# Layer 0's preparation in a score bank, and GpSimd splitting the maxima, in a two-layer gated cross-attention kernel

## The chip, the cores and the metric

The kernel runs on one core of one Trainium2 chip. The metric is the time of one execution on the device in microseconds. 2429.8 us is the median of three runs of the kernel before.

## What is computed

Two layers, each a cross-attention followed by a mixture of experts, over 32 batches of 56 query tokens of width 128 and 1500 context tokens. The attention of layer 0 has 32 heads of width 4 (16 pairs, whose outputs are subtracted), that of layer 1 has 16 heads of width 8 and a mask. Cut to what matters here:

```
x = x + tanh(g_xattn[0]) * L0_xattn(layernorm(x), ctx, ctx)
x = x + tanh(g_ffn[0])   * L0_ffn(layernorm(x))
x = x + tanh(g_xattn[1]) * L1_xattn(layernorm(x), ctx, ctx, mask)
x = x + tanh(g_ffn[1])   * L1_ffn(layernorm(x))

L0_xattn:  q = query @ Wq.T; k = ctx @ Wk.T; v = ctx @ Wv.T
           p = softmax(q * SCALE @ k.T) per head (32 heads, 1500 keys)
           attn = p1 @ v - lam * (p2 @ v), divided by its root mean square per head, @ Wp.T + bp
```

All numbers are kept nearly exact: a float32 value goes to TensorE as a high and a low float16 part.

## The kernel before, in words

`attend` (line 476) writes the attention of a layer for all engines, with an order laid down by hand. For a batch n of layer 0 it goes through 12 steps t of 125 keys each. A step consists of:

- the **scores** (`scores`, line 894) in two halves h of 16 heads each, 8 matmuls in all, into `score_ps[0]` and `score_ps[1]` (two banks each); the row maximum is subtracted by two extra rows of the operands;
- the exponentials on ScalarE (`exps`, line 1007), one instruction of 125x896 for each half, out of `score_ps` into `probs`;
- the **weighing** of the values (`weigh`, line 916) with the exponentials of the step before, in two halves i, into `acc_ps`, which holds the sum over all keys until ScalarE copies it out (`copy_output`, line 1015) in step 0 of the next batch;
- the **search** of the maxima of a later batch (`search`, line 880): 4 pieces of 112 queries by 500 keys in two pairs, each into one bank; VectorE reduces each to a column (`reduce_piece`, line 1056). 48 pieces make the maxima of a batch;
- one **preparation** (`use`, line 838, emptied by `drain`, line 979) for another batch: T turns a third of the context (n+3), K projects a third of the keys (n+3), V a third of the values (n+2), M transposes the maxima (n+1), F turns half of the output and A transposes the finished attention (n-1). K, T and the like are emptied by ScalarE; M is split into its high and low part by VectorE (lines 1043 and 1045).

The table `where` (line 553) says in which step, and on which side of the second search pair, a preparation stands. TensorE's order in a step is: both halves of the scores, first search pair, half of the weighing, preparation, second search pair, the other half of the weighing.

Searches and preparations share three banks, `spare_ps`, `max_ps[0]` and `max_ps[1]`, strictly in turn (`rooms`, line 593; `room`, line 597). A user waits until the user three places ahead has been emptied (`wait_for_room`, line 832):

```python
                k = place_of[user]
                if k >= len(rooms):
                    pe.wait_ge(*drained(order[k - len(rooms)]))
```

GpSimd prepares queries, splits context and keys into parts, and combines the outputs of the batch before (`finish`, line 771) once VectorE has written the reciprocals, which it does one step after the second F. SP issues the transfers in one queue: among them the transfer of the maxima into their two operand rows (`fill_m`, line 664, 4 transfers), behind the store of the context parts and ahead of that of the keys. The scores of step 0 of a batch wait for these rows (line 898).

Layer 1 runs the same code with half the heads (one half of scores, 2 pieces a step) and a mask.

## Time and profile before

| | |
|---|---|
| runs shown | 2422.18, 2429.8, 2433.78 us |
| the profiled execution | 2424.42 us; span from first to last instruction 2422.6 us |
| TensorE busy | 2235.1 us, 92% of the span |
| VectorE, ScalarE, GpSimd busy | 71%, 61%, 51% |
| granted TensorE clock, mean | 0.949 of 2.4 GHz |
| layer 0's attention | from about 100 to 1300 us of the span |

The profile lists for each engine what it executed and when, counted in us from the span's start. A stretch of it can be asked for in order of time. Consecutive instructions of one kind are merged there into one row with their number; the duration of such a row reaches to the end of its last. Matmuls are pipelined, and their ends are modelled, so that neighbouring rows of TensorE overlap; what can be read from them best is the distance from start to start. An idle time in brackets is that of the engine just ahead of the row, with what ended it.

### The profile page before, as it was taken

The page shows a single profiled execution, that of the slowest core. Times are in us where ns is not written, and L with a number is a line of the kernel's source. Part 1 is how long each engine was busy: PE and PEld are TensorE (multiplying, and loading weights), DVE is VectorE, ACT ScalarE, POOL GpSimd, SP SyncE. Part 2 cuts the span into 40 slices and gives each one's busy share as a digit, 9 for nine tenths or more (in the row PEclk, how much of TensorE's full clock was granted, in tenths as well). Part 3 has the DMA queues.
Part 4 walks back from the last instruction along what each step waited for, and adds up shares of the span by engine and source line. Part 5 has one row for each costly group of instructions (what it writes and reads, how often), then busy time and mean ns, then how long its engine had stood idle before and what let it go on. Part 6 is the DMA issues. An engine that isn't in the chain of part 4 may idle for free. (4 is left out here: it accounts for less than half of the span.)

```text
span 2422.6 us, 67012 instructions
## 1 busy us (share of the span) xinstructions
PE 2235.1 (92%) x27256; PEld 1258.2 (52%) x27256; DVE 1720.9 (71%) x3761; ACT 1484.6 (61%) x2101; POOL 1247.5 (51%) x1322
## 2 busy tenths in 40 slices
PE   3899999999999999999996986999999999999798
PEld 2344444444444444444444763566666655666576
DVE  3778888888888888888872554766777766775544
ACT  3167777777777777777774432566777666767322
POOL 5234545545455454454523344666777666773232
PEclk9589999999999999999997996899999999999799
DMA  3624343443444434434311006666676675762100
GB/s 108 128 71 103 88 92 103 87 105 85 99 103 93 92 98 92 104 85 94 91 13 51 23 29 135 125 133 130 141 142 137 136 137 122 142 136 41 53 1 15
DMA packets 113419, 227.80 MB, mean 94 GB/s; under 512 B 46052, under 2 KB 58596, under 8 KB 112612
## 3 DMA queue, kind: packets, MB, share of 16 engines
q1 hardware_dynamic: 113124, 223.67, 41.8%
q8 instruction: 209, 3.42, 0.7%
q14 instruction: 86, 0.70, 0.1%
HBM read 146.77 MB, written 76.48 MB: 92 GB/s over the span
## 5 line engine op out<-in xcount | busy, mean ns | idle before, releaser
L1012 ACT ACTIVATE probs<-score_ps 125x896 f32<-125x896 f32 x1152 | 1014.1, 916 | 368.9 <-PE score_ps L911 368.0
L1070 DVE TENSOR_REDUCE max_part<-max_ps 112x1 f32<-112x500 f32 x1023 | 665.4, 672 | 129.9 <-PE max_ps L890 89.9
L927 PE MATMUL acc_ps<-probs,vext 125*32 125x224 f32 (+1 forms) x12288 | 680.5, 317 | 4.3 <-issue 3.6
L890 PE MATMUL max_ps<-kstack,qstack 48*112 48x500 f16 x1534 | 512.3, 407 | 23.8 <-ACT kstack L987 11.1
L1067 DVE CUSTOM_DVE_ANT_0 kstack<-max_ps,kstack 112x500 f32<-112x500 f32 x511 | 335.3, 675 | 142.2 <-PE max_ps L890 83.4
L927 PEld LDWEIGHTS acc_ps<-probs,vext 125*32 125x32 f32 x12288 | 258.7, 109 | 272.9 <-issue 266.3
L1070 DVE TENSOR_REDUCE max_part<-spare_ps 112x1 f32<-112x500 f32 x513 | 344.8, 672 | 78.2 <-PE max_ps L890 45.6
L911 PE MATMUL score_ps<-qstack,kstack 50*125 50x224 f16 (+1 forms) x6144 | 389.8, 244 | 4.3 <-ACT probs L1012 2.1
L911 PEld LDWEIGHTS score_ps<-qstack,kstack 50*125 50x125 f16 x6144 | 306.4, 135 | 154.2 <-issue 122.4
L890 PE MATMUL spare_ps<-kstack,qstack 48*112 48x500 f16 x770 | 312.4, 406 | 30.0 <-issue 16.7
L767 POOL CAST khl<-kstack 128x500 f16<-128x500 f32 x189 | 113.6, 601 | 350.4 <-ACT kstack L994 194.1
L890 PEld LDWEIGHTS max_ps<-kstack,qstack 48*112 48x112 f16 x1534 | 168.0, 129 | 150.9 <-DVE max_part L1070 88.4
L1067 DVE CUSTOM_DVE_ANT_0 kstack<-spare_ps,kstack 112x500 f32<-112x500 f32 x257 | 173.5, 675 | 85.1 <-PE max_ps L890 77.1
L769 POOL TENSOR_TENSOR khl<-kstack,khl 128x500 f16<-128x500 f32 x189 | 202.2, 1070 | 15.1
L784 POOL TENSOR_TENSOR heads_out<-turned,rden 56x64 f32<-56x64 f32 x192 | 55.5, 289 | 241.2 <-DVE rden L1053 231.2
L1396 POOL TENSOR_TENSOR kstack<-kstack,probs 112x512 f32 (+1 forms) x68 | 90.6, 1333 | 171.2 <-DVE probs L1343 171.2
L905 PE MATMUL score_ps<-kstack 56*125 56x448 f16 x768 | 158.5, 402 | 0.2 <-issue 0.2
L747 POOL TENSOR_SCALAR kstack<-mask_in 112x1500 bf16<-112x1500 uint8 x31 | 147.2, 4747 | 2.6
L744 POOL TENSOR_SCALAR kstack<-mask_in 120x1500 f16<-120x1500 uint8 x31 | 147.8, 4768 | 0.0
L890 PEld LDWEIGHTS spare_ps<-kstack,qstack 48*112 48x112 f16 x770 | 99.0, 129 | 92.1 <-DVE max_part L1070 42.6
L736 POOL TENSOR_TENSOR qstack<-qrows,wide 112x896 f16<-112x896 f16 (+1 forms) x64 | 83.8, 1310 | 47.4 <-DMA qrows<-q_parts 25.4
L1243 PEld LDWEIGHTS max_ps<-kstack 128*112 128x112 f32 x896 | 104.4, 177 | 5.1 <-issue 0.2
(203 smaller groups left out, 2621.8 us busy)
## 6 DMA issues: line engine op xcount, KB each, us to landing
kstack<-k_parts SPq DMA_DIRECT2D x384, 187.5 KB, 6.6
k_parts<-khl SPq DMA_DIRECT2D x128, 375.0 KB, 2.8
ctx_f<-in_ctx SPq DMA_DIRECT2D x32, 750.0 KB
ctx_f<-context_parts SPq DMA_DIRECT2D x32, 750.0 KB, 4.5
context_parts<-ctx_f SPq DMA_DIRECT2D x16, 750.0 KB, 3.4
context_parts<-kstack SPq DMA_DIRECT2D x16, 750.0 KB, 3.3
mask_in<-in_mask SPq DMA_DIRECT2D x128, 82.0 KB
qrows<-q_parts SPq DMA_DIRECT2D x384, 7.0 KB, 7.4
```

What stands on the lines that cost most here:

```text
L744: nc.gpsimd.tensor_scalar(by_chunk(mask_f[n % SLOTS][0:HALF + SQ, :]), turned_keys(mask_in[0:HALF + SQ, :]), -BIG, None, ALU.mult).then_in ...
L747: nc.gpsimd.tensor_scalar(by_chunk(mask_add[n % SLOTS]), turned_keys(T["mask_in2"][:, :]), -BIG * BIG, None, ALU.mult).then_inc(s_add, 1)
L767: nc.gpsimd.tensor_copy(khl[:, 0, k], key_f[:, k]).then_inc(s_kp, 1)
L769: nc.gpsimd.tensor_tensor(khl[:, 1, k], key_f[:, k], khl[:, 0, k], ALU.subtract).then_inc(s_kp, 1)
L890: nc.tensor.matmul(room(("P", n, p))[0:PIECE, 0:TK], qstack[n % SLOTS][rows, c, PIECE * i:PIECE * (i + 1)], kstack[n % SLOTS][rows, c, TK ...
L905: nc.tensor.matmul(buf[0:KT, r, 0:448], mask_f[n % SLOTS][HALF * r:HALF * r + SQ, keys], big_eye[HALF * r:HALF * r + SQ, :], start=True, s ...
L911: last = nc.tensor.matmul(buf[0:KT, r, GC * k:GC * (k + 1)], kstack[n % SLOTS][rows, h * here + k, keys], qstack[n % SLOTS][rows, h * here ...
L927: last = nc.tensor.matmul(acc_ps[32 * j:32 * j + 32, TT * S * i:TT * S * (i + 1)].rearrange("p (s c) -> p s c", s=S), vext[n % SLOTS][:, t ...
L1012: nc.scalar.activation(probs[t % 2][:, 896 * h:896 * h + 896].rearrange("k (b c) -> k b c", b=2), score_ps[(t * H + h) % 2][0:KT, :, 0:448 ...
L1067: nc.vector.tensor_tensor_reduce(masked_scores[p % 2], scores, mask_add[n % SLOTS][:, TK * third:TK * third + TK], 1.0, -3.0e38, ALU.add, ...
L1070: nc.vector.reduce_max(best, scores, AX.X).then_inc(s_red, 1)
L1243: last = nc.tensor.matmul(bank[4 + e % DB - (0 if gated else 1)][0:TT, D * t:D * t + D], hidden[(e * NF + f) % HS][:, TT * t:TT * t + TT], ...
```

## The change

Only layer 0 is touched:

- All preparations of layer 0 stand behind the second search pair and ahead of the second half of the weighing. Each writes into one of the two banks of the score buffer of its own step's first half (`in_scores`), once that half's exponentials have been read out, and no longer takes a turn in the three rotating banks. Step 0 has none; T, F, T, F, T, K stand one step later than before, M and V share step 7, A and V step 11.
- The second half of the scores comes behind the first search pair. It waits until the preparation of the step before has been emptied. In odd steps the halves swap (`halves_of`), so that the first half of a step takes the buffer of the second half of the step before, and waits for both exponentials of that step.
- In step 0 both halves of the weighing come ahead of the second search pair.
- The transposed maxima are copied out by ScalarE, scaled, into a strip of `mask_in2`, which layer 0 does not use; GpSimd splits them in three instructions, behind the first third of the key split. `fill_m` waits for that.

```diff
-        where = {("T", 0): (0, 1), ("F", 0): (1, 1), ("T", 1): (2, 1), ("F", 1): (3, 1), ("T", 2): (4, 1), ("K", 0): (5, 1),
-                 ("V", 0): (6, 1), ("M", 0): (7, 1), ("K", 1): (8, 1), ("V", 1): (9, 1), ("K", 2): (10, 1), ("V", 2): (11, 1),
-                 ("A", 0): (11, 2)}
+        where = {("T", 0): (1, 1), ("F", 0): (2, 1), ("T", 1): (3, 1), ("F", 1): (4, 1), ("T", 2): (5, 1), ("K", 0): (6, 1),
+                 ("M", 0): (7, 1), ("V", 0): (7, 1), ("K", 1): (8, 1), ("V", 1): (9, 1), ("K", 2): (10, 1), ("A", 0): (11, 1),
+                 ("V", 2): (11, 1)}
...
+    spare_uses, in_scores = list(first_preps) + [("M", 0, 0)], {}
     for n in range(B):
         for t in range(NKT):
-            order += searched(n, t, 0) + at_step(n, t, 1) + searched(n, t, 1) + at_step(n, t, 2)
+            middle, last = at_step(n, t, 1), at_step(n, t, 2)
+            spare_uses += middle + last
+            if H == 2:
+                in_scores.update({user: n * NKT + t for user in middle})
+                middle = []
+            order += searched(n, t, 0) + middle + searched(n, t, 1) + last
...
+    def halves_of(step):
+
+        return (0, 1) if step % 2 == 0 or H == 1 else (1, 0)
 
     def room(user):
 
         if user in place_of:
             return rooms[place_of[user] % len(rooms)]
+        if user in in_scores:
+            return score_ps[halves_of(in_scores[user])[0]][:, int(user[0] in "MA"), :]
...
             def fill_m(n):
-                sp.wait_ge(s_mr, n + 1)
+                sp.wait_ge(s_mr, n + 1 if L.masked else 3 * (n + 1))
...
+            def split_max(n):
+                pool.wait_ge(s_mc, n + 1)
+                high, low = max_rows[0:L.tiles, 0, 0:PIECE], max_rows[0:L.tiles, 1, 0:PIECE]
+                nc.gpsimd.tensor_copy(high, max_f).then_inc(s_mr, 1)
+                pool.wait_ge(s_mr, 3 * n + 1)
+                nc.gpsimd.tensor_tensor(max_rest, max_f, high, ALU.subtract).then_inc(s_mr, 1)
+                pool.wait_ge(s_mr, 3 * n + 2)
+                nc.gpsimd.tensor_scalar(low, max_rest, BIG, None, ALU.mult).then_inc(s_mr, 1)
...
                 if n + 3 < B:
-                    split_keys(n + 3)
+                    split_keys(n + 3, range(1))
+                if L is L0 and n + 1 < B:
+                    split_max(n + 1)
+                if n + 3 < B:
+                    split_keys(n + 3, range(1, NTHIRD))
...
+                if user in in_scores:
+                    pe.wait_ge(s_exp, in_scores[user] * H + 1)
...
-            def scores(n, t, h):
-                number = (n * NKT + t) * H + h
-                at_least(pe, s_exp, number - 1)
-                if t == 0 and h == 0:
+            def scores(n, t, place):
+                step = n * NKT + t
+                number = step * H + place
+                h = halves_of(step)[place]
+                if L.masked:
+                    at_least(pe, s_exp, number - 1)
+                elif place == 0:
+                    at_least(pe, s_exp, number)
+                else:
+                    at_least(pe, s_exp, number - 2)
+                    for user in in_scores:
+                        if in_scores[user] == step - 1:
+                            pe.wait_ge(*drained(user))
...
-                    for h in range(H):
-                        scores(n, t, h)
+                    weighed = (n, t - 1) if t else (n - 1, LAST)
+                    scores(n, t, 0)
                     search(searched(n, t, 0))
+                    if H == 2:
+                        scores(n, t, 1)
                     for i in range(2):
-                        if t:
-                            weigh(n, t - 1, i)
-                        elif n:
-                            weigh(n - 1, LAST, i)
-                        if i == 0:
+                        if i == 1 and (t or H == 1):
+                            search(searched(n, t, 1))
                             for user in at_step(n, t, 1):
                                 use(user)
-                            search(searched(n, t, 1))
+                        if weighed[0] >= 0:
+                            weigh(*weighed, i)
+                    if t == 0 and H == 2:
+                        search(searched(n, t, 1))
...
+                if kind == "M":
+                    at_least(act, s_mr, 3 * n)
+                    nc.scalar.activation(max_f, spare_ps[0:L.tiles, 0:PIECE], ACT.Copy, scale=1.0 / BIG).then_inc(s_mc, 1)
```

How this moves instructions. First TensorE in step 8 of batch 1, which prepares keys, and the start of step 9. The names are those of the banks and buffers with their numbers: `score_ps` rows of 125x224 are scores, rows of 112x500 searches, `acc_ps` rows the weighing, and the row of 128x500 x3 the keys. Before:

```order
L911 MATMUL score_ps0<-qstack1,kstack1 125x224 x4
L911 MATMUL score_ps1<-qstack1,kstack1 125x224 x4
L890 MATMUL spare_ps<-kstack0,qstack0 112x500
L890 MATMUL max_ps0<-kstack0,qstack0 112x500
L927 MATMUL acc_ps<-probs1,vext1 32x224 x4
L857 MATMUL max_ps1<-ctx_f,w_parts 128x500 x3
L890 MATMUL spare_ps<-kstack0,qstack0 112x500
L890 MATMUL max_ps0<-kstack0,qstack0 112x500
L927 MATMUL acc_ps<-probs1,vext1 32x224 x4
```

With the change:

```order
L954 MATMUL score_ps0<-qstack1,kstack1 125x224 x4
L923 MATMUL max_ps1<-kstack0,qstack0 112x500
L923 MATMUL spare_ps<-kstack0,qstack0 112x500
L954 MATMUL score_ps1<-qstack1,kstack1 125x224 x4
L970 MATMUL acc_ps<-probs1,vext1 32x224 x4
L923 MATMUL max_ps0<-kstack0,qstack0 112x500
L923 MATMUL max_ps1<-kstack0,qstack0 112x500
L890 MATMUL score_ps0<-ctx_f,w_parts 128x500 x3
L970 MATMUL acc_ps<-probs1,vext1 32x224 x4
```

The fourth search shares its bank with the second one of its step before (`max_ps0`), and with the first one in the change (`max_ps1`). The keys leave the rotating banks for the bank of the first scores.

Second, TensorE at the start of a batch, steps 0 and 1 of batch 2 (the rows of 128x125 x4 turn the context). Before:

```order
L878 MATMUL max_ps0<-wide,attn_n 128x56
L911 MATMUL score_ps0<-qstack2,kstack2 125x224 x4
L911 MATMUL score_ps1<-qstack2,kstack2 125x224 x4
L890 MATMUL max_ps1<-kstack0,qstack0 112x500
L890 MATMUL spare_ps<-kstack0,qstack0 112x500
L927 MATMUL acc_ps<-probs1,vext1 32x224 x4
L848 MATMUL max_ps0<-wide,ctx_f 128x125 x4
L890 MATMUL max_ps1<-kstack0,qstack0 112x500
L890 MATMUL spare_ps<-kstack0,qstack0 112x500
L927 MATMUL acc_ps<-probs1,vext1 32x224 x4
```

With the change:

```order
L954 MATMUL score_ps0<-qstack2,kstack2 125x224 x4
L923 MATMUL spare_ps<-kstack0,qstack0 112x500
L923 MATMUL max_ps0<-kstack0,qstack0 112x500
L954 MATMUL score_ps1<-qstack2,kstack2 125x224 x4
L970 MATMUL acc_ps<-probs1,vext1 32x224 x8
L923 MATMUL max_ps1<-kstack0,qstack0 112x500
L923 MATMUL spare_ps<-kstack0,qstack0 112x500
L954 MATMUL score_ps1<-qstack2,kstack2 125x224 x4
```

Step 0 has no preparation any more, its weighing is in one piece, and two searches with nothing but four scores between them and the next two end it.

Third, GpSimd between the combination of a batch's output and the next preparation of queries: the splits of the last third of the context and of the keys, before:

```order
L798 TENSOR_TENSOR attn_n<-attn,rms 56x128
L756 CAST ctx_f<-kstack 128x500
L758 TENSOR_TENSOR ctx_f<-kstack,ctx_f 128x500
L767 CAST khl<-kstack 128x500
L769 TENSOR_TENSOR khl<-kstack,khl 128x500
L767 CAST khl<-kstack 128x500
L769 TENSOR_TENSOR khl<-kstack,khl 128x500
```

With the change, the numbers of the buffers written out:

```order
L823 TENSOR_TENSOR attn_n<-attn,rms 56x128
L772 CAST ctx_f<-kstack0 128x500
L774 TENSOR_TENSOR ctx_f<-kstack0,ctx_f 128x500
L792 CAST khl<-kstack1 128x500
L794 TENSOR_TENSOR khl<-kstack1,khl 128x500
L779 CAST max_rows<-mask_in2 16x112
L781 TENSOR_TENSOR mask_in2<-mask_in2,max_rows 16x112
L783 TENSOR_SCALAR max_rows<-mask_in2 16x112
L792 CAST khl<-kstack1 128x500
L794 TENSOR_TENSOR khl<-kstack1,khl 128x500
```

Three small instructions stand behind the first third of the keys; the two that VectorE had for this are gone from its order.

## Rows read from the trace of the kernel before

**Rows 1.** Busy time by stretch, one batch: us, then PE, PEld, DVE, ACT, POOL, clock

```profile
608.35:645.77 37.42, 36.37 (x406) 17.30 (x407) 31.04 (x54) 27.15 (x37) 18.66 (x27) 1.00 0.37 96
```

**Rows 2.** In order of time, PE, a step with keys: start, us, work

```profile
602.24 0.60 PE L911 MATMUL score_ps<-qstack,kstack 50*125 50x224 f16 x8
602.68 0.37 PE L890 MATMUL max_ps<-kstack,qstack 48*112 48x500 f16 x1
...
602.98 0.58 PE L927 MATMUL acc_ps<-probs,vext 125*32 125x224 f32 x8
603.50 0.81 PE L857 MATMUL max_ps<-kstack,w_parts 128*128 128x500 f16 x3
604.24 0.41 PE L890 MATMUL max_ps<-kstack,qstack 48*112 48x500 f16 x1
604.40 0.41 PE L890 MATMUL spare_ps<-kstack,qstack 48*112 48x500 f16 x1
604.75 0.59 PE L927 MATMUL acc_ps<-probs,vext 125*32 125x224 f32 x8
605.26 0.60 PE L911 MATMUL score_ps<-qstack,kstack 50*125 50x224 f16 x8
```

**Rows 3.** In order of time, ACT: exponentials, the last two rows five steps apart

```profile
602.69 1.73 ACT L1012 ACTIVATE probs<-score_ps 125x896 f32<-125x896 f32 x2 [0.67 <-PE score_ps L911]
...
615.72 1.73 ACT L1012 ACTIVATE probs<-score_ps 125x896 f32<-125x896 f32 x2 [0.96 <-PE score_ps L911]
...
630.83 1.73 ACT L1012 ACTIVATE probs<-score_ps 125x896 f32<-125x896 f32 x2 [0.67 <-PE score_ps L911]
```

**Rows 4.** In order of time, PE: values, then context, each with the search behind it

```profile
606.52 0.91 PE L864 MATMUL spare_ps<-w_parts,ctx_f 128*125 128x128 f16 x12
607.36 0.48 PE L890 MATMUL max_ps<-kstack,qstack 48*112 48x500 f16 x2
...
616.53 0.65 PE L848 MATMUL max_ps<-wide,ctx_f 125*128 125x125 f32 x4
617.11 0.42 PE L890 MATMUL max_ps<-kstack,qstack 48*112 48x500 f16 x1
```

**Rows 5.** In order of time, DVE: the second reduction of the step in rows 2

```profile
603.68 0.67 DVE L1070 TENSOR_REDUCE max_part<-spare_ps 112x1 f32<-112x500 f32 x1
```

**Rows 6.** In order of time, ACT and PE, step 1 of a batch

```profile
612.01 0.58 ACT L987 ACTIVATE kstack<-spare_ps 128x500 f32<-128x500 f32 x1
...
612.64 0.41 PE L890 MATMUL spare_ps<-kstack,qstack 48*112 48x500 f16 x1 [0.61 <-ACT kstack L987]
```

**Rows 7.** In order of time, PE, near the end of layer 0's attention

```profile
1266.36 0.41 PE L911 MATMUL score_ps<-qstack,kstack 50*125 50x224 f16 x4 [0.20 <-ACT probs L1012]
1266.70 0.96 PE L927 MATMUL acc_ps<-probs,vext 125*32 125x224 f32 x16
1267.59 0.27 PE L878 MATMUL max_ps<-wide,attn_n 56*128 56x56 f32 x1
```

**Rows 8.** In order of time, ACT, the last batch

```profile
1276.55 13.71 ACT L1012 ACTIVATE probs<-score_ps 125x896 f32<-125x896 f32 x16 [0.27 <-PE score_ps L911]
```

**Rows 9.** In order of time, POOL: the combination, and the key split behind it

```profile
623.77 1.40 POOL L784 TENSOR_TENSOR heads_out<-turned,rden 56x64 f32<-56x64 f32 x4 [3.96 <-DVE rden L1053]
625.27 0.60 POOL L791 TENSOR_SCALAR attn<-heads_out,lam_s 56x128 f32<-56x128 f32 x1
...
634.04 1.07 POOL L769 TENSOR_TENSOR khl<-kstack,khl 128x500 f16<-128x500 f32 x1
```

**Rows 10.** In order of time, SP's queue: the rows of the maxima

```profile
633.83 3.07 SPq L670 DMA_DIRECT2D qstack<-max_rows  x4
```

**Rows 11.** DMA issues of the page: count, KB each, median us to landing

```profile
kstack<-k_parts SPq DMA_DIRECT2D x384, 187.5 KB, 6.6
k_parts<-khl SPq DMA_DIRECT2D x128, 375.0 KB, 2.8
...
qrows<-q_parts SPq DMA_DIRECT2D x384, 7.0 KB, 7.4
```

More of the change, by code:

```diff
@@ L533, in attend @@
     s_mr = sem(L.name + "_max_split")
+    s_mc = s_mr if L.masked else sem(L.name + "_max_copied_out")
+    max_f, max_rest = (T["mask_in2"][0:L.tiles, 4 * PIECE * i:4 * PIECE * (i + 1)].bitcast(F32) for i in range(2))
     s_os = sem(L.name + "_output_copied")
@@ L758, in split_context, with split_keys @@
                 nc.gpsimd.tensor_tensor(ctxT[n % 2][:, 1, k], context_f[:, k], ctxT[n % 2][:, 0, k], ALU.subtract).then_inc(s_cp, 1)
-            def split_keys(n):
-                for i in range(NTHIRD):
+            def split_max(n):
[6 more added lines that the diff above has]
+                nc.gpsimd.tensor_scalar(low, max_rest, BIG, None, ALU.mult).then_inc(s_mr, 1)
+            def split_keys(n, thirds=range(NTHIRD)):
+                for i in thirds:
                     k = slice(TK * i, TK * i + TK)
@@ L814, in _ @@
             split_keys(2)
+            if L is L0:
+                split_max(0)
             for n in range(B):
@@ L980, in drain @@
                 kind, n, i = user
-                if kind == "M":
+                if kind == "M" and L.masked:
                     return
@@ L1017, in copy_output @@
                 nc.scalar.activation(out_sb[:, 0:L.o_cols], acc_ps[:, 0:L.o_cols], ACT.Copy).then_inc(s_os, 1)
-            for user in first_preps:
+            for user in first_preps + [("M", 0, 0)]:
                 drain(user)
@@ L1037, in drain @@
                 kind, n, i = user
-                if kind != "M":
+                if kind != "M" or not L.masked:
                     return
```

16 lines of the change are left out of this document (10 added, 6 removed).

## The prediction, made before the changed kernel had run

> **What bounds the kernel now.** I read the stretches first, then one batch of layer 0 on TensorE, ScalarE and VectorE in order of time, then GpSimd, the DMA queue and the stage's end. The edit touches only layer 0's attention; layer 1 gets the same instructions in the same order, as do the norms and the feed-forwards, so their time is taken as unchanged. In one batch (12 steps) TensorE is busy 36.37 of 37.42 us, VectorE 31.04, ScalarE 27.15, at a granted clock of 1.00, the 2.4 GHz level [rows 1]. That reads like "TensorE is full", and it misleads. Follow the step that prepares keys [rows 2]: scores 602.24, first search pair 602.68, half of the weighing 602.98, keys 603.50, then the second pair as two separate starts, 604.24 and 604.40, weighing 604.75, next scores 605.26: 3.02 us. ScalarE's pairs of exponentials show the same length for five steps in a row, 615.72 to 630.83 being 15.11 [rows 3], though their preparations differ: on TensorE the keys take 0.74, the values 0.84, turning the context 0.58 [rows 2, 4]. A constant length with unequal contents is a loop, not a full engine. The loop: four users share three banks, so a preparation pushes the fourth search of a step (604.40, in spare_ps) onto the bank of the step's second search. It starts 0.05 after that one's reduction ends, 603.68 + 0.67 = 604.35 [rows 5]. Add it up: 0.35 to the weighing, 0.51 to the next scores, 0.44 to the next pair, some 0.4 until that is in its bank, two reductions of 0.6 to 0.67, and the next fourth search may start: 3.0 us. All other work lies in the loop's slack.
>
> Twice in a batch it is worse. In step 1 the first search waits 0.61 idle for ScalarE, which empties its bank of the context turned in step 0 only at 612.01, behind the copy of the accumulator [rows 6]. In step 7 the transposed maxima hold a bank until VectorE has split them. What these two and the transpose of the attention cost is 37.42 - 12 x 3.02 = 1.2.
>
> **The change, part by part, for one batch.** *Banks.* The three rotating banks hold searches alone. The fourth search then waits for the first one's reduction, 0.6 earlier, and no search waits for ScalarE. What is late next is TensorE itself, so its starts must be summed. *Split scores.* Eight scores and a pair took 0.44 + 0.30 before the weighing [rows 2]. Now: half of the scores, 0.22; the pair ahead of the other half, not in the trace, nearest the pair ahead of the weighing, 0.30; four scores ahead of a weighing, 1266.36 to 1266.70, 0.34 [rows 7]. That is 0.86 for 0.74. Bounds: nothing extra, since the streams are the same; or a full change of work at both new seams. What such a change costs: both weighing halves together take 0.89 (1266.70 to 1267.59), two apart 2 x 0.52, so 0.15 [rows 2, 7]; then 0.74 + 0.30 = 1.04. I stay with the nearest rows, 0.86. *The rest of a step.* Weighing half 0.52; second pair ahead of the preparation 0.35, as 604.40 to 604.75; preparation; weighing half 0.51: with the 0.86, 2.24 without preparation. Eleven of these are 24.6. Three keys, three values, three contexts at 0.74, 0.84, 0.58 and two output turns, taken like the context, are 2.2 + 2.5 + 2.9 = 7.6. The transposes of maxima and attention are single matmuls of 0.27 [rows 7], pipelined: between 0 and 0.27 each, 0.1 taken. Step 0, without preparation: 0.86 + 0.52 + 0.51 + 0.30 = 2.2. But VectorE needs 31.04 / 48, 0.63 a reduction, 2.5 for its four, and step 0's second pair comes behind both weighing halves, so step 1's first searches find banks unread: some 0.6 of waiting. Sum 24.6 + 7.6 + 0.2 + 2.2 + 0.6 = 35.2. I add 0.3 for small waits that a sum of starts does not see, and take **35.5 us for 37.42**, 1.9 less.
>
> *ScalarE* gains one copy of 16x112. Exponentials start 0.45 after the scores, two take 1.73, a drain 0.58 [rows 2, 3, 6]: 2.3 to 2.6 of steps of 2.8 to 3.1. Two new waits. A preparation waits for the first exponentials of its own step, done at 0.45 + 0.9 = 1.4 (a little over half of the 1.73); TensorE comes at 0.86 + 0.52 + 0.35 = 1.7: nothing, margin 0.3. The second half of the scores waits for the preparation's drain, done 3.1 to 3.2 after its step's start and wanted at 2.8 to 3.1 plus 0.52: nothing, margin 0.2 to 0.3. Both are thin, and TensorE's whole queue would stand behind them.
>
> *VectorE* loses the split of the maxima and its wait. It isn't the bound, and the wait in step 7 is already left out of the sum.
>
> *The first scores of a step* wait for both exponentials of the step before, where one sufficed, since the halves swap banks. Cycle: 1.73 + 0.05 + 0.45 = 2.2 us, covered as long as VectorE's 2.5 bounds a step. Not covered in the last 17 steps, in which nothing is searched (5 of batch 30, 12 of batch 31): there ScalarE runs 16 exponentials in 13.71, 1.71 a step [rows 8]. Up to 17 x 0.5 = 8.7 is lost; some of these steps are longer already by output turns and a copy, so 7 is taken.
>
> *GpSimd and the queue.* The second output turn moves from step 3 to step 4, so the reciprocals come in step 5, by the sum some 16.3 after the batch's start. From the start of the combination to the end of the first third of the key split it takes 634.04 + 1.07 - 623.77 = 11.3 [rows 9], to 27.6. Then the three new instructions of 16x112: none like them is in the trace; nothing up to the 0.60 of the 56x128 row each [rows 9], 1.5 taken with their links, the upper end: 29.1. On SP stand behind them four row transfers, 3.07 to issue [rows 10], the last at 31.6, and then the key store, which needs the last third and isn't delayed. Their landing is not in the trace: 2.8 for the key store and 7.4 for the query rows bound it [rows 11]. The 7.4 stand behind six key fills; these have one context store ahead of them, so I take 2.8: 34.4. The next batch's scores come at 35.5: nothing, with 1 us to spare where 6.7 were (633.83 + 2.5 + 2.8 against 645.77). The other two thirds of the key split move back by 1.5, into idle time.
>
> *Total.* Batches 1 to 28 are full ones: 28 x 1.9 = 53. Batch 0 runs partly at the lower clock level and batch 29 has few preparations; nothing is taken for them. 2424.4 - 53 + 7 = 2378 against the profiled execution; the median of the runs shown is 5 us higher and would give 2384. **Forecast: 2380 us.**
>
> **Rivals.** (a) *The split costs nothing.* For: a pair follows eight scores after 0.44, and the 0.22 of four is just half of that. Against: the pair ahead of the weighing takes 0.30 where a preparation hides nothing of it. It would be 0.12 x 12 = 1.4 less, 34.1 a batch: 2424 - 28 x 3.3 + 7 = 2339. The Trainium skill (TensorEngine Tiling, Key Properties) says that changing the tiling mode, not just the tile, drains the engine. By that rule the split is free, as scores (50 rows) and searches (48 rows) lie in the same halves of the array. No row here shows the new seam itself.
>
> (b) *The seams eat it.* With 1.04 for 0.86 a batch is 35.5 + 2.2 = 37.7, and TensorE is the bound it seems to be: 2424 + 8 + 7 = 2439; with half of that, 2408. For: busy 36.4 of 37.4. Against: the constant 3.02.
>
> (c) *The maxima come late, and it is slower than before.* Their path now ends on GpSimd behind the combination. If the last row lands 7.4 after its issue, at 39.0, the scores of each batch wait 3.5, and a batch is 39.0: 2424 + 28 x 1.6 + 7 = 2476. It costs from a landing of 3.9 on and turns the sign near 5.5. For: the margin shrinks from 7 to 1, and a 7.4 exists. Against: that one has 1.1 MB of key fills ahead of it.
>
> **How the numbers follow.** Forecast case 0.62, (a) 0.12, (b) 0.14, (c) 0.12. A measurement of this kernel tells 0.5%, 12 us, from no change. Faster by more: 0.62 + 0.12 + a third of (b) = 0.78; within: 0.07; slower: (c) and the far end of (b), 0.15. The forecast's own range is 2362 to 2400 (35.0 to 36.2 a batch). For 8 in 10 the range reaches to (a) and into (b), 2335 to 2430, and leaves (c) out.
>
> **What would show it.** Accumulator copies 35.5 us apart; steps of unequal length by their preparation, 2.8 for the context, 3.0 to 3.1 for keys and values; no search waiting for ScalarE, and few for reductions outside steps 0 and 1; the split on GpSimd followed at once by four row transfers, and the first scores of a batch without a gap; ScalarE idle 0.5 a step in the last 17. Equal steps near 3 us would mean a new loop. A gap ahead of a batch's first scores is (c). Unequal steps, each 0.15 longer than summed, are (b).

## The result, and the profile after

The changed kernel takes 2349.4 us, the median of 4 runs (2344.1 to 2361.7), and the kernel before beside it 2426.0 (4 runs): a ratio of 0.970, 95% interval 0.968 to 0.972. The profiled execution took 2361.7 us, the longest of the four, with a span of 2359.2, beside 2424.4 and 2422.6 before. A batch of layer 0, read from one copy of the accumulator to the next, is 35.01 us where it was 37.42. The figure that decides below is this batch length: within one profile of the changed kernel it repeats to 0.02 us, while the totals of single runs differ by several us. The window of one batch, columns as in [rows 1]:

```profile
610.04:645.05 35.01, 34.84 (x408) 18.66 (x404) 29.61 (x51) 27.93 (x39) 19.66 (x30) 1.00 0.45 102
```

TensorE is busy in 34.84 of 35.01 us, almost as in [rows 1], although the batch is 2.4 us shorter. Its row looks the same when it is full and when it stands in a loop. In order of time, TensorE, one step with a context third (step 3), then the first reductions of that step on VectorE:

```profile
618.27 0.41 PE L954 MATMUL score_ps<-qstack,kstack 50*125 50x224 f16 x4
618.51 0.37 PE L923 MATMUL spare_ps<-kstack,qstack 48*112 48x500 f16 x1
618.51 0.37 PE L923 MATMUL max_ps<-kstack,qstack 48*112 48x500 f16 x1
618.73 0.35 PE L954 MATMUL score_ps<-qstack,kstack 50*125 50x224 f16 x4
619.01 0.58 PE L970 MATMUL acc_ps<-probs,vext 125*32 125x224 f32 x8
619.53 0.41 PE L923 MATMUL max_ps<-kstack,qstack 48*112 48x500 f16 x1
619.65 0.41 PE L923 MATMUL spare_ps<-kstack,qstack 48*112 48x500 f16 x1
620.00 0.65 PE L881 MATMUL score_ps<-wide,ctx_f 125*128 125x125 f32 x4
620.58 0.58 PE L970 MATMUL acc_ps<-probs,vext 125*32 125x224 f32 x8
621.09 0.41 PE L954 MATMUL score_ps<-qstack,kstack 50*125 50x224 f16 x4
```

```profile
618.92 0.68 DVE L1119 TENSOR_REDUCE max_part<-spare_ps 112x1 f32<-112x500 f32 x1 [0.37 <-PE max_ps L923]
619.52 1.25 DVE L1119 TENSOR_REDUCE max_part<-max_ps 112x1 f32<-112x500 f32 x2
```

Three things stand here. The scores, the pair and the other scores take 0.24, 0.22 and 0.28 us, 0.74 to the weighing, exactly as long as eight scores and a pair in [rows 2]. The two searches of the second pair start 0.12 apart, since the fourth waits for the first reduction (618.92 + 0.68 = 619.60). From the pair's start to the preparation it is 0.47. The steps are no longer equal: in order from step 0, with what TensorE prepares in each,

| | 0 | 1 | 2 | 3 | 4 | 5 | 6 | 7 | 8 | 9 | 10 | 11 |
|---|---|---|---|---|---|---|---|---|---|---|---|---|
| before | T 3.14 | F 3.84 | T 3.03 | F 3.02 | T 3.02 | K 3.02 | V 3.03 | M 3.23 | K 3.02 | V 3.02 | K 3.02 | V, A 3.03 |
| after | 2.22 | T 3.21 | F 2.80 | T 2.82 | F 2.80 | T 2.83 | K 2.99 | M, V 3.20 | K 2.99 | V 3.08 | K 2.99 | A, V 3.08 |

Step 1 keeps two waits: 0.17 of its first scores for the exponentials, and one of its second search, for the reduction that empties its bank. TensorE, where the duration 0.77 of the two searches shows that they don't start together, and VectorE's reduction, which ends at 612.81:

```profile
612.26 0.41 PE L954 MATMUL score_ps<-qstack,kstack 50*125 50x224 f16 x4 [0.17 <-ACT probs L1061]
612.51 0.77 PE L923 MATMUL max_ps<-kstack,qstack 48*112 48x500 f16 x2
612.86 0.61 PE L954 MATMUL score_ps<-qstack,kstack 50*125 50x224 f16 x4
```

```profile
612.13 0.68 DVE L1119 TENSOR_REDUCE max_part<-max_ps 112x1 f32<-112x500 f32 x1 [0.17 <-PE spare_ps L923]
```

GpSimd and then SP's queue, the split of the maxima, answering to [rows 9, 10]:

```profile
637.42 0.27 POOL L779 CAST max_rows<-mask_in 16x112 f16<-16x112 f32 x1
637.76 0.39 POOL L781 TENSOR_TENSOR mask_in<-mask_in,max_rows 16x112 f32<-16x112 f32 x1
638.24 0.49 POOL L783 TENSOR_SCALAR max_rows<-mask_in 16x112 f16<-16x112 f32 x1
```

```profile
638.75 2.69 SPq L685 DMA_DIRECT2D qstack<-max_rows  x4
```

The split ends 28.7 us into the batch (638.73), the rows are issued until 641.4, and the scores that need them start at 645.05 with no gap. In the last 17 steps ScalarE, which ran through the last eight without a pause in [rows 8], now stops 0.50 us in most, and 0.26 to 0.39 where it also empties a preparation:

```profile
1214.91 1.73 ACT L1061 ACTIVATE probs<-score_ps 125x896 f32<-125x896 f32 x2 [0.50 <-PE score_ps L954]
```

By the accumulator's copies: the first stands at 162.5 before and 157.0 after; from there 28 batches take 1047.3 and 980.3 us, 67.0 less; the three intervals to the last copy 81.6 and 87.1, 5.6 more; from the last copy to the end, in which nothing was changed, 1131.3 and 1134.8. In the other kernels of this study that keep the new preparation banks, this last part is 1121.5 to 1139.0, so some 9 us either way say nothing of the edit.

### The profile page after: what moved, and what is told of

Read it like the earlier page. It is cut to its first block and busy times, and to the rows that moved or that the text cites. A ratio compares the mean times of both kernels' runs of the same rounds, so it can differ in the third digit from the quotient of the medians.

```text
span 2359.2 us, 67435 instructions
## 1 busy us (share of the span) xinstructions
PE 2192.7 (93%) x27256; PEld 1303.0 (55%) x27256; DVE 1677.1 (71%) x3697; ACT 1507.8 (64%) x2133; POOL 1278.9 (54%) x1418
## 5 line engine op out<-in xcount | busy, mean ns | idle before, releaser
L1119 DVE TENSOR_REDUCE max_part<-max_ps 112x1 f32<-112x500 f32 x1024 | 654.7, 668 | 115.3 <-PE spare_ps L923 68.3
L970 PE MATMUL acc_ps<-probs,vext 125*32 125x224 f32 (+1 forms) x12288 | 673.2, 316 | 6.6 <-issue 6.1
L954 PE MATMUL score_ps<-qstack,kstack 50*125 50x224 f16 (+1 forms) x6144 | 454.8, 244 | 17.2 <-ACT probs L1061 13.9
L954 PEld LDWEIGHTS score_ps<-qstack,kstack 50*125 50x125 f16 x6144 | 344.4, 134 | 183.8 <-issue 122.2
L923 PEld LDWEIGHTS max_ps<-kstack,qstack 48*112 48x112 f16 x1535 | 173.5, 129 | 143.4 <-issue 77.7
L1044 ACT ACTIVATE vext<-score_ps 125x512 f32<-125x512 f32 x102 | 60.9, 597 | 78.6 <-PE score_ps L897 78.2
```

The source lines that it names most:

```text
L923: nc.tensor.matmul(room(("P", n, p))[0:PIECE, 0:TK], qstack[n % SLOTS][rows, c, PIECE * i:PIECE * (i + 1)], kstack[n % SLOTS][rows, c, TK ...
L954: last = nc.tensor.matmul(buf[0:KT, r, GC * k:GC * (k + 1)], kstack[n % SLOTS][rows, h * here + k, keys], qstack[n % SLOTS][rows, h * here ...
L970: last = nc.tensor.matmul(acc_ps[32 * j:32 * j + 32, TT * S * i:TT * S * (i + 1)].rearrange("p (s c) -> p s c", s=S), vext[n % SLOTS][:, t ...
L1119: nc.vector.reduce_max(best, scores, AX.X).then_inc(s_red, 1)
```

## The experiments

Each batch below is the distance of two accumulator copies in the middle of layer 0. Single times stand beside a kernel before of 2419 to 2425 us. e1 to e8 ran once each, e9 to e12 four to six times. The exchange of the halves and the undivided weighing of step 0 are in every kernel below that has the new banks, and in none that has the old ones, so that their own worth isn't measured.

### The parts of the change, alone and left out

**e1: VectorE splits the maxima, as before.**

```
             def drain(user):
...
-                if kind == "M" and L.masked:
+                if kind == "M":
...
-                if kind != "M" or not L.masked:
+                if kind != "M":
```

The first pair of lines is ScalarE's, which empties M no more, the second VectorE's, which splits it; GpSimd's `split_max` is not called for layer 0, and VectorE does its part behind the second reductions of step 7.

> The changed kernel, with the split of the maxima given back to VectorE (two instructions, placed behind the second reduction pair of step 7), straight from the score bank. Theory (the gain is the broken loop between reductions and searches): VectorE has 0.4 to 0.7 us of idle time in each step, 0.7 ahead of step 8, so two instructions of 0.25 fit; a batch stays at 35.0 us (34.9 to 35.2), total within 5 us of the changed kernel. Rival (taking VectorE's work away is part of the gain): a batch of 35.5 or more. The row transfers should issue about 5 us earlier in the batch, without effect.

Measured: batch 35.00, total 2356.5; the row transfers begin about 2.5 us earlier in the batch, not 5, without effect. Whether GpSimd or VectorE splits them is worth nothing once the maxima lie in a bank that no search waits for.

**e2: the kernel before, with the preparation behind the second pair, banks still in turn.**

```
                         if i == 0:
+                            search(searched(n, t, 1))
                             for user in at_step(n, t, 1):
                                 use(user)
-                            search(searched(n, t, 1))
```

The turns of the three banks and VectorE's order of emptying them follow TensorE's.

> The kernel before, with one edit: each preparation stands behind the second search pair instead of ahead of it, still in the three rotating banks; scores together as before. Theory: the fourth search then waits for the first reduction, but the scores still stand ahead of the first pair and only half of the weighing between the pairs, so that this reduction ends some 0.3 us after TensorE comes for the fourth search, and the preparation no longer fills that time: steps of about 3.0 (context, output) and 3.2 to 3.3 (keys, values), a batch of 37.0 to 37.8, no gain. Rival (the place of the preparation is what gains): a batch near 35.3, as changed.

Measured: batch 40.04, total 2504.2. The rival, a gain from the place alone, is out; the loss is larger than the theory's range. TensorE, a step with keys:

```profile
622.21 0.42 PE L890 MATMUL spare_ps<-kstack,qstack 48*112 48x500 f16 x1
622.54 0.41 PE L890 MATMUL max_ps<-kstack,qstack 48*112 48x500 f16 x1
623.12 0.81 PE L857 MATMUL max_ps<-kstack,w_parts 128*128 128x500 f16 x3 [0.17 <-DVE max_part L1070]
```

Two users wait now, each for one reduction more: the fourth search 0.33 behind the third, and then the keys, which on VectorE's row are released by two reductions that run from 621.80 for 1.26, to 623.06. In the kernel before, the 0.74 of the keys passed while the first reduction ran; with the preparation last that cover is gone. A step with keys is 3.42.

**e3: the change without the split of the scores.**

```
                     scores(n, t, 0)
-                    search(searched(n, t, 0))
                     if H == 2:
                         scores(n, t, 1)
+                    search(searched(n, t, 0))
```

> The changed kernel, with one edit: both halves of the scores ahead of the first search pair, as before; score banks for the preparations, their places and the rest stay. Theory (the second half between first pair and weighing is needed to give VectorE time for the first reduction): the fourth search waits about 0.3 us in each step, a batch of 36.8 to 37.5, nearly all of the gain gone. Rival (the score banks alone give the gain, the split costs nothing and brings nothing): 35.0 to 35.3.

Measured: batch 38.11, total 2448.9: slower than the kernel before, and a larger loss than the theory's 36.8 to 37.5. TensorE, and the drain on ScalarE that it waits for:

```profile
607.00 0.73 PE L954 MATMUL score_ps<-qstack,kstack 50*125 50x224 f16 x8
607.54 0.37 PE L923 MATMUL spare_ps<-kstack,qstack 48*112 48x500 f16 x1
...
608.39 0.41 PE L923 MATMUL max_ps<-kstack,qstack 48*112 48x500 f16 x1
608.69 0.41 PE L923 MATMUL spare_ps<-kstack,qstack 48*112 48x500 f16 x1
```

```profile
606.60 0.59 ACT L1042 ACTIVATE kstack<-score_ps 128x500 f32<-128x500 f32 x1 [0.70 <-PE score_ps L890]
```

Without the split the second scores want the preparation's bank 0.22 us after the step's start, at 607.22. It is empty at 607.19, but TensorE goes on some 0.14 behind such an end (in e5 a drain ends at 1203.71 and its scores start at 1203.85), so 0.1 is lost: scores and search take 0.54 where they took 0.44. The pair comes late, so its reduction ends late, and the fourth search waits 0.30. The split covers both.

**e4: the change with the preparation ahead of the second pair.**

> The changed kernel, with one edit: the preparation ahead of the second search pair, as before, still in the score bank. Theory: it then waits some 0.1 to 0.2 us for the first exponentials of its step, and the fourth search no longer waits 0.12 for the first reduction; the two nearly cancel: a batch of 35.0 to 35.5. Rival (the place behind the second pair is essential): 36 or more.

Its edit exchanges `search(searched(n, t, 1))` with the loop over `at_step(n, t, 1)` in steps with t > 0. Measured: batch 35.49, total 2366.4. The fourth search waits no more (both start at 608.07), but the preparation comes 0.56 behind the weighing and a search of the first pair 0.08 behind the other, and from the scores to the weighing it is 0.86 (605.92 to 606.78) for 0.74. The place behind the second pair is worth 0.5 us a batch of the 2.4.

**e11: the kernel before with the split alone.**

```
-                    for h in range(H):
-                        scores(n, t, h)
-                    search(searched(n, t, 0))
+                    scores(n, t, 0)
+                    search(searched(n, t, 0))
+                    if H == 2:
+                        scores(n, t, 1)
```

> The kernel before with one edit only: the second half of the scores behind the first search pair. Preparations keep their rotating banks and their place ahead of the second pair. Theory (the constant 3.02 us step was a loop: fourth search, weighing, next scores, next first pair, its second reduction, fourth search; the reductions count from when the first pair stands in its banks): the first pair starts 0.22 us sooner after the scores' start, so the loop is 2.80 us and TensorE's own sum takes over where that is longer (keys 2.86 to 2.9, values 2.95 to 3.0, context and output turns 2.8 from the loop); steps 1 and 7 keep their waits, 1.2 us in all; a batch is 35.3 to 36.0 us, and the total 2360 to 2385 us. Rival (the change's gain needs the preparations out of the rotating banks; a split alone only moves the wait): steps stay at 3.02 and the batch at 37.2 us or more, the total at 2415 to 2430.

Measured: batch 36.99; total 2409.0 (6 runs), ratio 0.994, 0.992 to 0.997. Neither was right on the sum: the rival had 37.2 or more and 2415 to 2430, the theory 35.3 to 36.0 and 2360 to 2385, and the result is nearer to the rival's. The steps are mostly the theory's. They are, from step 0, 3.40, 3.85, 2.83, 2.83, 2.84, 2.86, 3.08, 3.30, 2.86, 3.08, 2.98, 3.08. TensorE, first the step with keys, then step 1 of the next batch:

```profile
616.86 0.41 PE L911 MATMUL score_ps<-qstack,kstack 50*125 50x224 f16 x4
617.10 0.37 PE L890 MATMUL max_ps<-kstack,qstack 48*112 48x500 f16 x1
...
618.12 0.81 PE L857 MATMUL max_ps<-ctx_f,w_parts 128*128 128x500 f16 x3
618.86 0.41 PE L890 MATMUL max_ps<-kstack,qstack 48*112 48x500 f16 x1
618.86 0.41 PE L890 MATMUL spare_ps<-kstack,qstack 48*112 48x500 f16 x1
...
619.72 0.41 PE L911 MATMUL score_ps<-qstack,kstack 50*125 50x224 f16 x4
...
641.50 0.41 PE L911 MATMUL score_ps<-qstack,kstack 50*125 50x224 f16 x4
642.71 0.42 PE L890 MATMUL max_ps<-kstack,qstack 48*112 48x500 f16 x2 [0.81 <-ACT kstack L988]
```

The second pair starts together at 618.86, where it stood apart at 604.24 and 604.40 in [rows 2]: an earlier first pair breaks the 3.02 loop, as the theory had it. What failed is the sum over the batch. I had added the excess of steps 0, 1 and 7 over 3.02 to shorter steps; but the release of a held bank sets those steps, whatever the others take (3.14, 3.84, 3.23 before; 3.40, 3.85, 3.30 here). In the changed kernel steps 0, 1 and 7 are 8.63 together against 10.55 here: 1.9 of the 2.0 us between the two kernels.

**e12: the kernel before with the first pair ahead of all scores.**

Its edit puts `search(searched(n, t, 0))` ahead of the loop over h.

> The kernel before with the first search pair ahead of both halves of the scores, nothing else. Theory: the pair starts 0.44 us sooner, the loop would be 2.58 us, and TensorE's own sum bounds all steps (keys 2.87, values 2.97, context 2.71); the waits of steps 1 and 7 stay (the first pair of step 1 meets ScalarE's drain 0.4 us earlier, so its wait is up to 1.0 instead of 0.61); a batch is 34.8 to 35.8 us, the total 2350 to 2380. Rival (with the pair first, it waits for the reductions of the step before, which the scores had covered): the batch is 36.5 us or more.

Measured: batch 38.97; total 2474.0 (4 runs), ratio 1.021, 1.017 to 1.026. The rival is right. TensorE, the first pair of a middle step, then a later row, that of step 1:

```profile
619.16 0.41 PE L890 MATMUL max_ps<-kstack,qstack 48*112 48x500 f16 x1
619.49 0.41 PE L890 MATMUL spare_ps<-kstack,qstack 48*112 48x500 f16 x1
619.49 0.80 PE L911 MATMUL score_ps<-qstack,kstack 50*125 50x224 f16 x8
...
630.41 0.41 PE L890 MATMUL spare_ps<-kstack,qstack 48*112 48x500 f16 x1 [1.14 <-ACT kstack L990]
```

In the middle step the second search finds its bank unread, 0.33 late, and the scores stand behind it in TensorE's order, so the exponentials wait as well; in step 1 it is 1.14, for ScalarE's drain of step 0.

Together, batches in us: before 37.42; split alone 36.99; bank and place without the split 38.11; bank and split with the preparation ahead of the second pair 35.49; all 35.01. Place alone, with the banks in turn, costs 2.6; bank and place cost 0.7 without the split, and with it they gain 2.0. So the gain is no sum of the parts' gains: the bank frees the searches, and with the split TensorE no longer waits for that bank (e3). The new banks alone, with the preparation in its old place and no split, weren't run.

### How near is the split of the maxima to the scores?

**e7: the maxima behind all thirds of the keys on GpSimd.** `split_keys(n + 3)` ahead of `split_max(n + 1)`, no third behind it.

> The changed kernel, but GpSimd splits the maxima after all three thirds of the keys instead of after the first. In the changed kernel this split ends 28.7 us into the batch and the rows' four transfers are issued until 31.4; the scores that need them start at 35.0 without a wait. It isn't known how much of the 3.6 us between is slack, since the landing isn't shown by a wait anywhere. Theory (the maxima's path has about 1 us to spare or less): the thirds end about 35 us into a batch, the rows are issued until 38 and land 1.5 to 3 us later, so the batch is 39.5 to 41 us and the total about 2480 to 2520; the scores of step 0 are then released by the transfer, and the gap gives the landing. Rival (the third splits are quick or the keys' thirds wait on something that moves with them, and the path has several us to spare): the batch stays below 37 us.

Measured: 2594.3 us, batches of 40.1 to 45.0, about half of them 44.3 to 44.4. The last instruction of the split on GpSimd; the scores on TensorE that the rows release; and windows, first of the gap a batch earlier and of the time behind it, then of a batch near 40:

```profile
635.74 0.49 POOL L783 TENSOR_SCALAR max_rows<-mask_in 16x112 f16<-16x112 f32 x1
```

```profile
640.13 0.41 PE L952 MATMUL score_ps<-qstack,kstack 50*125 50x224 f16 x4 [3.99 <-DMA qstack<-max_rows]
```

```profile
591.80:595.70 3.90, 0.00 (x0) 0.00 (x0) 0.00 (x0) 0.11 (x1) 1.73 (x2) 1.00 0.05 16
...
597.00:609.00 12.00, 12.00 (x84) 4.95 (x78) 6.89 (x12) 6.23 (x9) 1.73 (x2) 0.50 0.78 118
...
426.00:429.00 3.00, 3.00 (x28) 1.40 (x25) 1.26 (x2) 2.23 (x3) 0.00 (x0) 0.50 0.69 221
```

From the end of the split (636.23) to the scores it is 3.90 us, issue included; the last of the four transfers is issued until 638.94 and is there 1.2 later. In the changed kernel the same 3.90 would end at 642.63, and the scores want it at 645.05: 2.4 us to spare. The batch is longer than the theory had it, since a second cost comes with the gap: TensorE stands still for 4.0 us, starts again at 595.78, and the granted clock is 0.67 from 596 to 597 and 0.50, the 1.2 GHz level, from 597 to 609, a search taking 0.66 in place of 0.41. That the rest of the time goes with this clock shows in a comparison of three batches whose gaps are alike and whose stretches at the low clock are not. From first scores to first scores, less the gap at the end and the 35.01 of a batch without one:

| first scores at | until | less the gap and 35.01 | clock low behind the first scores |
|---|---|---|---|
| 425.46 | 465.99 | 1.5 us | 3.4 us |
| 508.93 | 551.42 | 3.5 us | 8.9 us |
| 595.78 | 640.13 | 5.4 us | 13.6 us |

### What is left in a step, and in the tail

**e5: the last 17 steps with their halves in turn, each waiting for its own bank.**

```
-        return (0, 1) if step % 2 == 0 or H == 1 else (1, 0)
+        return (0, 1) if step % 2 == 0 or H == 1 or step >= tail else (1, 0)
...
+                elif step >= tail:
+                    at_least(pe, s_exp, number - 1)
```

> The changed kernel, but in the last 17 steps, which have no search and no preparation, the two halves of the scores are not exchanged, and each half waits only for the exponentials that last read its own bank (and for the drain of a preparation of the step before that used it). In the changed kernel these steps take 2.22 us each with ScalarE idle 0.50 us in each, since the first scores wait for both exponentials; before the change they took 1.71. Theory (that wait is what the tail lost): the batch stays at 35.0 us, the last 17 steps come back to 1.71 us (1.7 to 1.8), and the program ends 17 x 0.51 = 8.7 us earlier against a profile with the same untouched stages; against the changed kernel's total 5 to 9 us less. Rival (the tail's steps are bound by the weighing that follows its own exponentials, and the exchange has nothing to do with it): steps stay at 2.2 us and the total is the same.

Measured: batch 35.01; the last interval between copies 22.56 in place of 26.20; total 2345.4. ScalarE in the last batch:

```profile
1208.76 12.09 ACT L1069 ACTIVATE probs<-score_ps 125x896 f32<-125x896 f32 x14 [0.59 <-PE score_ps L962]
```

Fourteen exponentials without a pause, 1.73 a step. The last two intervals are 4.3 us shorter together, less than the 8.7 expected: ScalarE still stops four times in the 17 steps, 0.59 three times and 1.16 once. TensorE shows what holds it:

```profile
1197.33 0.60 PE L962 MATMUL score_ps<-qstack,kstack 50*125 50x224 f16 x8 [0.76 <-DMA qstack<-max_rows]
...
1203.85 0.60 PE L962 MATMUL score_ps<-qstack,kstack 50*125 50x224 f16 x8 [0.26 <-ACT turned L1059]
```

The 1.16 is the arrival of the last batch's maxima. The other three stand behind the emptying of a preparation: with the halves in turn the first scores of a step use the bank that the preparation of the step before had.

**e6: the first search pair ahead of both halves of the scores**, in the changed kernel.

> The changed kernel, but the first search pair of a step goes ahead of both halves of the scores, so that the order on TensorE is pair, scores, scores, weighing, pair, preparation, weighing. Theory (what is left in a step beside TensorE's own work is the 0.12 us that the fourth search waits for the first reduction): the first reduction starts 0.24 us earlier, the wait is gone, a step of keys takes 2.85 to 2.90 us instead of 2.99, and the batch 33.5 to 34.3 us; the total is some 20 to 40 us less. What could take it back: the exponentials start 0.2 us later in the step and the weighing, or the next step's first scores, then wait for them; then the batch is 35.0 or more and the rows show scores or weighing released by ScalarE in most steps. Rival (the fourth search's wait is not time lost, TensorE's own order bounds a step): 35.0.

Measured: batch 34.16, total 2324.4. TensorE, a step with keys:

```profile
616.56 0.41 PE L923 MATMUL max_ps<-kstack,qstack 48*112 48x500 f16 x1
616.57 0.41 PE L923 MATMUL spare_ps<-kstack,qstack 48*112 48x500 f16 x1
616.94 0.81 PE L890 MATMUL score_ps<-kstack,w_parts 128*128 128x500 f16 x3
...
618.19 0.42 PE L923 MATMUL max_ps<-kstack,qstack 48*112 48x500 f16 x2
618.45 0.55 PE L954 MATMUL score_ps<-qstack,kstack 50*125 50x224 f16 x8
618.93 0.58 PE L970 MATMUL acc_ps<-probs,vext 125*32 125x224 f32 x8
619.44 0.41 PE L923 MATMUL spare_ps<-kstack,qstack 48*112 48x500 f16 x1
619.45 0.41 PE L923 MATMUL max_ps<-kstack,qstack 48*112 48x500 f16 x1
```

The fourth search stands beside the third again and the step is 2.88 for 2.99. Ten steps give 1 us, and step 1 takes some back (its first pair waits 0.56 for VectorE). The same edit that cost 1.5 us a batch with the banks in turn (e12) gives 0.85 here. It also shows the price of the split once more: a pair and then eight scores take 0.26 + 0.48 = 0.74.

**e8: the preparations in the steps of the kernel before**, one of them in step 0.

> The changed kernel, but with the preparations in the steps of the kernel before: the first context transposition in step 0, the values in step 6, the maxima in step 7, behind the second pair in step 0 too. It tests the words that step 0 has none. In step 0 ScalarE has the output copy besides both exponentials, and the first scores of step 1 already wait 0.17 us for ScalarE. Theory (a preparation in step 0 costs there what it saves in another step, because its drain is one more turn of ScalarE that the second scores of step 1 wait for): step 0 or step 1 gets 0.3 to 0.6 us longer, the step that had two preparations 0.3 us shorter, and the batch is 34.8 to 35.3 us. Rival (keeping step 0 free costs a whole step's worth nowhere, the drain is hidden): the batch is 34.5 or less. Other rival (the drain collides with the copy and the exponentials in a chain): 35.6 or more.

Measured: batch 34.84, total 2356.4. Steps 0 and 1 are 2.57 and 3.10, 0.24 more than in the changed kernel, and step 7, which has M alone, is 2.51; the other ten steps together are 0.40 shorter. A step 0 without any preparation isn't worth its room: the difference is 0.17 us a batch, which the totals can't tell.

**e9: e5 and e6 together, step 1 alone in the changed kernel's order.**

> The changed kernel with the first search pair of each step ahead of both halves of the scores (as in e6), step 1 alone kept in the changed kernel's order, and the last 17 steps with the halves in turn and their own waits (as in e5). Theory (each of the two stalls is a cost of its own, so they add): the search's steps stay at e6's 2.69 to 2.88 us, step 1, whose first pair waited 0.56 us for VectorE in e6, gets 0.1 to 0.3 us shorter since scores stand where that wait was, the batch is 33.9 to 34.1 us, the last 17 steps take 1.71 to 1.75; total 2312 us (2305 to 2322), the ratio to the kernel before 0.955. Rival (step 1 waits for ScalarE or VectorE either way): the batch stays at 34.15 us and the total is 2316.

Measured: batch 34.05, last interval 22.55; total 2326.4, the median of 5 runs (2317.0 to 2327.3), ratio to the kernel before 0.958, 0.955 to 0.960. The changed kernel stands at 0.968 to 0.972: this version beats both. From the first to the last copy it takes 1036.1 us, the changed kernel 1067.4. The total came out above the range that was expected, because I had started from e6's single execution, whose part behind the last copy was 1121.5 us; here it is 1131.8.

Step 1 still stops, 0.39 for ScalarE's exponentials.

**e10: e9 with the preparations where e8 has them.**

> As e9, with the preparations in the steps of the kernel before (as in e8: one in step 0, none in a step twice but the maxima, which share step 7 with nothing, and the last two in step 11). In e8 that gave 0.16 us a batch. Theory (the gain there is a preparation's change of work in a shared step, independent of the order of pair and scores): 0.1 to 0.2 us a batch less than e9, 3 to 5 us in all, total about 2308 us. Rival (with the pair first in step 0, its drain is what the second scores of step 1 wait for, longer than the 0.16 us seen in e8): the same as e9 or up to 5 us more.

Measured: batch 34.03; total 2329.8 (5 runs), ratio 0.960, 0.958 to 0.963. The rival is right: with the pair first the 0.17 of e8 shrinks to 0.02, and the totals don't differ.

## Why the prediction was right, and where its terms were not

**The loop.** Right, and shown: e11 changes nothing but when the first pair starts against the scores, and the constant 3.02 falls apart into 2.83 to 3.08 by preparation. "Steps of unequal length by their preparation" holds in the changed kernel: 2.80 to 2.83 where 2.8 was named, 2.99 and 3.08 where 3.0 to 3.1. *What is late next is TensorE itself* is right only nearly: the fourth search waits 0.12 for the first reduction in most steps, where the prediction had few waits for reductions outside steps 0 and 1, and e6 gets that back.

**The seam.** Sized wrong, 0.86 for a measured 0.74. Rival (a) had this mechanism: the split costs nothing, and nothing was paid in e6's order either. These rows agree with the Trainium skill (TensorEngine Tiling, Key Properties), by which changing the tiling mode, not just the tile, drains TensorE: scores and searches, 50 and 48 rows in the same halves of the array, follow each other at 0.22 to 0.24. The nearest row of before, a pair ahead of a weighing, contained another kind of seam.

**The second pair.** Sized wrong the other way: 0.35 was taken to the preparation, 0.47 it is. The two errors are 0.12 each, one per step, and cancel: 1.21 is exactly what was forecast for 0.86 + 0.35. Rival (a)'s mechanism came true while its 34.1 us didn't, for this reason.

**The allowance.** The sum of the starts was 35.2, measured are 35.01. The 0.3 for "small waits that a sum of starts does not see" wasn't needed; the small wait that existed was hidden in the seam's error. Steps 0 and 1 came out at 5.43 for 5.6, and M and A at 0.12 and 0 for 0.1 each. In the sum, the price of a reduction was given as 0.63, but 31.04 / 48 is 0.65 and holds VectorE's other work too; reductions in a row start 0.60 apart (618.92 and 619.52). The allowance is 0.3 of the 0.5 us by which a batch was missed, steps 0 and 1 are most of the rest, and 28 x 0.5 = 14 us are most of the miss against the profiled execution.

**ScalarE's margins.** The preparation's wait for the first exponentials and the second scores' wait for the drain were costed at nothing with 0.2 to 0.3 to spare. In the step of 626.72, keys are wanted at 628.46 and the exponentials end near 628.07; the drain ends at 629.89 and the scores are wanted at 630.16. Right, and e3 shows what is behind the thinner one. The first scores' wait for both exponentials was said to be covered outside the last 17 steps: in step 1 it isn't, 0.17.

**The tail.** Forecast 7 us, found 5.6, of which e5 got back 4.3; the mechanism, first scores that wait for both exponentials, is shown by that.

**GpSimd and the rows.** The split ends at 28.7 us for 29.1. Its landing, bounded by 2.8 and 7.4 and taken as 2.8 behind the start of the last issue, is 1.8 by e7 (638.31 to 640.13), and the batch is 0.5 shorter, so 2.4 us were to spare in place of 1. Rival (c) is out here, but e7 shows that its price is higher than it was worked out, by the clock.

**The total.** The forecast was 2380 us, 2378 against the profiled execution; that took 2361.7. Of the 17 us between, 14 are the shorter batches, 1.4 the tail, and 5.5 an earlier first copy, against 3.5 more in the untouched rest (and 0.6 of rounding and of what lies around the span). Most of the earlier first copy is not shown to be the change's. It lies at 157.0 to 162.8 in the changed kernel's relatives (164.9 in e7, with its gap), and at 160.8 to 162.5 in three of the four kernels with the old banks, and it follows the moment at which the clock rises in batch 0: from 126 to 130 the granted clock is 0.82 in the changed kernel and 0.50 in the kernel before, which has 0.84 only from 138 to 142. e1, with TensorE's order as in the changed kernel, has 0.50 to 138 and 0.85 from 138 to 142 as well, and its first copy stands at 161.1. The median lies 12 us below the profiled execution, which the untouched part's spread of 1121.5 to 1139.0 us covers.

The gain in medians is 77 us where 46 to 50 were forecast, and 2349.4 lies outside the forecast's own range of 2362 to 2400, in whose lowest corner the batch of 35.01 is. It lies inside the wide one, 2335 to 2430, which reached so far down for rival (a), and it is nearer to that rival's 2339 than to 2380. The total couldn't have told the two; the steps did. What was right is the loop, the lengths of the steps and the waits that were costed at nothing; that 0.86 + 0.35 came out to the hundredth is luck, by two errors that cancel.

## What to carry to other kernels

A constant step length with unequal contents is a loop of waits even where the engine reads 97% busy; find the one user that comes late, follow it round, and sum its starts. Expect the parts of such an edit to depend on each other: pair first cost 2% with banks in turn and won with them freed, and the new bank without the split was slower than no change. An allowance on top of a sum of starts was wrong here; name the wait instead. And when an isolated irregular step exceeds the loop's length, treat it as a length of its own that won't shrink with the others.

## What the runs showed of the hardware

Changing between two kinds of matmul in the same halves of the array cost nothing that shows (0.74 split or not), while from one half of the weighing (32-column tiles) to the next there were 0.15 us to pay when other work stood between [rows 2, 7]. Four small transfers of rows took 3.9 us from the end of their producer to the release of TensorE, 2.7 of it their issue one behind the other on SP (e7). With each of three 4.0 to 4.3 us stops of TensorE that were followed in e7, the granted clock fell to 0.50, once before the stop had ended (0.80 from 507 to 508, scores at 508.93) and twice within 1.3 us of its end, and stayed there for 3.4, 8.9 and 13.6 us of the time behind the stop, in which TensorE was busy; each us of it cost about 0.4, so that the longest made a 4.0 us stop cost 9.3. The stops of 0.6 us in the kernel before, 0.8 in e11 and 1.1 in e12, one in each batch, left it at 1.00 from 300 to 1100 us.
